# One core, a three-layer graph network: the engine and the place in the order at which edge attributes are split into bf16 parts

## The chip, the cores and the metric

The kernel runs on one core of a Trainium2 chip. The metric is the device time of one execution in microseconds. The kernel before takes 2959.71 us (median of three runs, 2949.01 to 2960.8).

## The reference

There are 12500 nodes with 64 features, and 212500 edges (200000 and one loop for each node), sorted by target `dst`, with 16 attributes each. Three layers of the same form are followed by a residual and a layer normalisation:

```python
def conv(h, W, b):
    m = jnp.concatenate([h[dst], h[src], edge_attr], axis=1) @ W + b
    return jax.ops.segment_sum(m, dst, num_segments=n_nodes)
h = relu(conv(x, W1, b1)); h = relu(conv(h, W2, b2)); h = conv(h, W3, b3)
out = layernorm(x + h)
```

Since `conv` is linear, a node needs three sums over its edges: of `h[src]`, of `edge_attr`, and the count. The sum of the attributes is the same in all three layers and is made once, in layer 0.

## The kernel before, in words

**Tiling.** The 12500 targets are 25 batches (`BATCHES`) of 500 nodes. Of a batch, 375 targets (`DENSE`) get their neighbours' sum as a product with a block of the adjacency matrix: for each of 100 tiles of 125 source nodes, `blocks[..., t, :]` holds the number of edges from those sources to the 375 targets in fp8. `apply_wide` (L1261) multiplies the high and middle bf16 parts of the features with it, `apply_narrow` (L1269) the low part; ten tiles are a unit. The remaining 125 targets ("far") are summed from gathered rows: 18 indirect DMAs of GpSimd (`gather_rows`, L712) fetch the source rows of 18 x 128 edges into `far_rows`, and `sum_far` (L1298, L1302) multiplies them with one-hot masks.

**Layer 0 builds the blocks.** While batch g is applied, batch g + 1 is built in 75 steps (`BUILDS`): VectorE makes a one-hot of 500 columns (`make_key`, L1018, a ring of 7 buffers), each fifth step also five small one-hots (`make_low`, L1008, two buffers), TensorE multiplies the two (`build_chunk`, L1241), and ScalarE copies the counts to fp8 (`keep_counts`, L796). Finished batches are stored to HBM (L804, 4.6 MB each) and read back in layers 1 and 2.

**Attributes.** In layer 0 each batch has six groups of edges, five near (75 targets, 128 x 11 edges) and one far (128 x 18 edges). SyncE loads a group's attributes and targets (`load_group`, four staging buffers), VectorE makes its mask (`make_mask`, L1026, `make_far_masks`, L1042), the fp32 attributes are split into three bf16 parts whose sum is the value, and TensorE sums them over the mask (`sum_attr`, L1288) after units 1, 3, 4, 6, 8 and 9. The split is `split_attr` on GpSimd, four instructions (L740 cast, L742 subtract, L744 cast, L746 subtract). It waits for the group's loads and for the sum two groups back, since `attr_parts` has two buffers. GpSimd's program alternates: a split, then three or four of the batch's 18 gathers (`GATHERS`).

**What orders VectorE.** Its program in layer 0 is one loop over the 75 steps n of the batch being built; small work for batches g and g - 1 is attached to fixed n: masks at 5, 25, 33, 48, 63, far masks at 18, 42, 57, `keep_acc` at 5 (it frees the PSUM bank that TensorE's next `apply_wide` waits for), `keep_attr` at 7, `keep_deg` at 12, `keep_h` at 32, and from 63 on the node steps: `take_nodes` (L1088) copies the convolution's result, four steps turn it into three parts.

**End of layer 0.** The gathers of layer 1 read rows of all nodes, so GpSimd waits for the stores of every batch's parts, the last of which follows batch 24's `sum_far`, its convolution and its node steps.

Of the kernel before, what the change touches and what calls it, by code (L numbers as in the profile page):

```python
# [5 lines left out]
def gnn_kernel(nc, x, src, dst, edge_attr, weights, out):  # L6
# [13 lines left out]
    ALU = mybir.AluOpType  # L20
# [4 lines left out]
    E, ED = edge_attr.shape  # L25
# [15 lines left out]
    NEAR = 5  # L41
    GW = DENSE // NEAR
    BUILDS = DENSE // W
# [12 lines left out]
    J = 11  # L56
    FJ = 18
    ROWS = [0, 112, L]
    PER_BATCH = NEAR + 1
# [24 lines left out]
    MASK_AT = [BUILDS * u // UNITS + 3 for u in SUM_AFTER[0:NEAR]]  # L84
    FAR_MASK_AT = [18, 42, 57]
    NODES_AT = [63, 66, 68, 70, 72]
    GATHERS = [FJ * k // NEAR for k in range(NEAR + 1)]
# [15 lines left out]
    with ctx:  # L103
# [432 lines left out]
        def landed_of(n):  # L536

            return sum(2 if m % PER_BATCH < NEAR else 1 for m in range(n % RING, n + 1, RING)) * DMA
# [133 lines left out]
        def _(pool):  # L672
# [58 lines left out]
            def split_attr(n):  # L731

                s, turn = n % RING, n % 2
                pool.wait_ge(attr_landed[s], landed_of(n))
                if n >= 2:
                    pool.wait_ge(attr_summed, n - 1)
                js = J if n % PER_BATCH < NEAR else FJ
                values = attr_stage[:, s, 0:js * ED].rearrange("p (j c) -> p j c", c=ED)
                into = [attr_parts[:, turn, 0:js, part * ED:(part + 1) * ED] for part in range(PARTS)]
                nc.gpsimd.tensor_copy(into[0], values).then_inc(attr_split, 1)  # L740
                pool.wait_ge(attr_split, n * PARTS + 1)
                nc.gpsimd.tensor_tensor(values, values, into[0], ALU.subtract).then_inc(attr_left, 1)  # L742
                pool.wait_ge(attr_left, n + 1)
                nc.gpsimd.tensor_copy(into[1], values).then_inc(attr_split, 1)  # L744
                pool.wait_ge(attr_split, n * PARTS + 2)
                nc.gpsimd.tensor_tensor(into[2], values, into[1], ALU.subtract).then_inc(attr_split, 1)  # L746

            for g in range(BATCHES):
                for k in range(PER_BATCH):
                    split_attr(g * PER_BATCH + k)  # L750
                    if k < NEAR:
                        for j in range(GATHERS[k], GATHERS[k + 1]):
                            gather_rows(g, j)
# [123 lines left out]
        def _(dve):  # L877
# [142 lines left out]

            def make_mask(b, k):
# [134 lines left out]
            for g in range(-1, BATCHES):  # L1156
                for n in range(BUILDS):
# [6 lines left out]
                    if g >= 0:  # L1164
                        if n == FIRST_MASK_AT:
# [280 lines left out]
```

## Time and profile before

| | |
|---|---|
| median of 3 runs | 2959.71 us |
| the profiled execution | 2963.69 us, its span 2961.8 us |
| mean granted TensorE clock | 0.981 |
| TensorE matmul busy | 2777.0 us, 94% of the span |
| VectorE busy | 1546.4 us, 52% |
| ScalarE busy | 1265.0 us, 43% |
| GpSimd busy | 2024.0 us, 68% |
| layer 0, steady batches | 200 to 1388 us of the span, 23 batches |

The busy shares are means over stages with different limits: VectorE is busy for nine tenths until about 1385 us and hardly at all later. Busy time of an instruction includes its end, which overlaps the next one's start, so start-to-start distances are shorter than durations. The stretch from 200 to 1388 us holds 23 of layer 0's 25 batches, from one `sum_far` to another.

### The profile page before, as it was taken

What the parts mean: (1) busy time and instruction counts of PE and PEld (TensorE: products, weight loads), DVE (VectorE), ACT (ScalarE), POOL (GpSimd) and SP (SyncE); (2) the same over time, 40 slices, a digit from 0 to 9 for tenths busy, and PEclk for the clock granted to TensorE, in tenths of its full rate; (3) what the DMA queues carried; (4) which work ended last, traced back from release to release, by engine and by line L of the source; (5) the groups of instructions that cost most, each with busy time, mean ns of one, the idle gap of its engine ahead of it and who ended that gap; (6) DMA issues with size and microseconds to landing.
All of it is one profiled execution on the core that took longest, in us unless ns stands there. A gap on an engine that the chain in (4) does not pass through costs nothing.

```text
span 2961.8 us, 60063 instructions
## 1 busy us (share of the span) xinstructions
PE 2777.0 (94%) x23143; PEld 1772.7 (60%) x23143; DVE 1546.4 (52%) x3237; ACT 1265.0 (43%) x2315; POOL 2024.0 (68%) x2141
## 2 busy tenths in 40 slices
PE   1499999999999999999859999999998999999998
PEld 0256666666666666666536666666665666666665
DVE  7999999999999999997201111111111212121211
ACT  2588898989889898986000000000000000000000
POOL 5277766676767767677277777777737777777773
PEclk9799999999999999999879999999999999999999
DMA  4353534445353444535958988888877899988882
GB/s 91 81 162 103 166 109 144 130 112 162 101 166 108 146 129 118 156 101 167 220 134 202 213 218 210 210 210 214 212 201 176 209 212 215 212 209 207 208 213 53
DMA packets 242618, 489.50 MB, mean 165 GB/s; under 512 B 156178, under 2 KB 191708, under 8 KB 214213
## 3 DMA queue, kind: packets, MB, share of 16 engines
q1 hardware_dynamic: 136846, 272.20, 34.8%
q10 hardware_dynamic: 58404, 143.10, 18.0%
q0 software_dynamic: 47088, 70.34, 12.2%
q8 instruction: 190, 3.11, 0.5%
q14 instruction: 90, 0.74, 0.1%
HBM read 341.80 MB, written 143.65 MB: 164 GB/s over the span
## 4 chain that ended last, share of the span: by engine, by line
PE 82%; DVE 5%; POOL 5%; issue 3%; DMA 2%; ACT 2%; SPq 1%; ACTq 0%; POOLq 0%; DVEq 0%
PE ps L1261 36%; PE ps L1269 20%; PE ps L1241 12%; POOL far_rows L712 4%; PE ps L1337 3%; PE ps L1298 3%; PE ps L1288 2%; PE ps L1338 2%; DVE is_key L1018 1%; PE ps L1302 1%; PE ps L1323 1%; ACT blocks L796 1%; DVE is_low L1008 1%; DMA parts<-in_x 1%; PE ps L1312 1%
## 5 line engine op out<-in xcount | busy, mean ns | idle before, releaser
L712 POOL DMA_INDIRECT far_rows<-parts,far_src x1350 | 1486.5, 1101 | 528.4 <-issue 382.1
L1261 PE MATMUL ps<-blocks,parts 125*128 125x375 fp8e4 x7500 | 1548.4, 324 | 4.0 <-ACT blocks L796 2.4
L796 ACT ACTIVATE blocks<-ps 125x505 fp8e4<-125x505 f32 x1875 | 1117.0, 756 | 149.0 <-PE ps L1241 146.2
L1261 PEld LDWEIGHTS ps<-blocks,parts 125*128 125x128 bf16 x7500 | 736.8, 100 | 421.3 <-issue 16.3
L1241 PE MATMUL ps<-is_key,is_low 128*125 128x505 bf16 x1875 | 707.9, 388 | 40.1 <-DVE is_key L1018 24.4
L1018 DVE TENSOR_SCALAR is_key<-from_one,parts 128x500 bf16<-128x500 f16 x1875 | 686.2, 413 | 3.0 <-PE ps L1241 1.2
L1269 PE MATMUL ps<-blocks,parts 125*64 125x375 fp8e4 x7500 | 686.6, 326 | 0.0
L1269 PEld LDWEIGHTS ps<-blocks,parts 125*64 125x64 bf16 x7500 | 399.0, 110 | 275.4 <-issue 154.4
L1115 DVE COPY z<-ps 125x256 f32<-125x256 f32 x51 | 21.6, 424 | 892.3 <-PE ps L1338 855.6
L1241 PEld LDWEIGHTS ps<-is_key,is_low 128*125 128x125 bf16 x1875 | 258.8, 139 | 226.8 <-DVE is_key L1018 51.5
L1042 DVE SCALAR_TENSOR_TENSOR far_masks<-far_dst,from_one 128x750 fp8e4<-128x750 int32 (+1 forms) x125 | 195.4, 1563 | 326.0 <-PE ps L1302 317.2
L1008 DVE TENSOR_TENSOR is_low<-from_one,parts 128x625 bf16<-128x625 f16 x375 | 307.1, 819 | 49.0 <-PE ps L1241 48.7
L740 POOL CAST attr_parts<-attr_stage 128x176 bf16<-128x176 f32 x150 | 72.1, 481 | 293.1 <-DMA dst_stage<-in_dst 150.2
L823 ACT ACTIVATE node_rows<-z,node_deg 125x64 f32<-125x64 f32 x200 | 54.0, 367 | 379.2 <-DVE z L1115 353.1
L855 ACT COPY acc_sb<-ps 128x500 f32<-128x500 f32 x50 | 28.8, 575 | 385.3 <-PE ps L1302 375.2
L863 ACT ACTIVATE std<-var,eps 125x4 f32<-125x4 f32 x25 | 7.4, 297 | 401.3 <-DVE var L1132 401.3
L857 ACT COPY own_sb<-ps 64x500 f32<-64x500 f32 x50 | 28.4, 568 | 279.9 <-PE ps L1323 279.9
L1298 PE MATMUL ps<-far_masks,far_rows 128*128 128x125 fp8e4 x1350 | 93.8, 224 | 51.2 <-DMA far_rows<-parts,far_src 51.2
L720 POOL TENSOR_SCALAR attr_stage<-attr_stage 128x256 f32<-128x256 f32 x150 | 136.9, 912 | 3.2
L1026 DVE SCALAR_TENSOR_TENSOR masks<-dst_stage,from_one 128x825 bf16<-128x825 int32 x125 | 128.9, 1032 | 8.4 <-DMA dst_stage<-in_dst 8.4
L1337 PE MATMUL ps<-w_src,acc_sb 128*125 128x64 f32 x600 | 124.0, 288 | 0.7 <-ACT own_sb L857 0.7
L1298 PEld LDWEIGHTS ps<-far_masks,far_rows 128*128 128x128 bf16 x1350 | 80.7, 100 | 68.4 <-issue 66.1
(120 smaller groups left out, 1423.2 us busy)
## 6 DMA issues: line engine op xcount, KB each, us to landing
blocks<-counts SPq DMA_DIRECT2D x100, 1066.4 KB
counts<-blocks ACTq DMA_DIRECT2D x25, 4101.6 KB
blocks<-counts SPq DMA_DIRECT2D x100, 984.4 KB
far_rows<-parts,far_src POOLq DMA_INDIRECT x1350
blocks<-counts SPq DMA_DIRECT2D x100, 123.8 KB
counts<-blocks ACTq DMA_DIRECT2D x25, 476.1 KB
blocks<-counts SPq DMA_DIRECT2D x100, 114.3 KB
attr_stage<-in_edge_attr SPq DMA_DIRECT2D x125, 88.0 KB, 1.9
```

The costliest lines, as they stand in the source:

```text
L712: nc.gpsimd.indirect_dma_start(far_rows[:, g % 2, j, :], None, parts_d[layer], bass.IndirectOffsetOnAxis(ap=far_src[:, g % BATCHES, j:j + ...
L720: nc.gpsimd.tensor_scalar(attr_stage[:, 3, 0:256], attr_stage[:, 1, 0:256], 1.0, None, ALU.mult).then_inc(rested, 1)
L796: nc.scalar.activation(blocks[0:L, b % 2, :, n * W:(n + 1) * W], build[0:L, c % BUILD, 0:COLS].rearrange("p (t w) -> p t w", w=W), ACT.Cop ...
L1008: nc.vector.tensor_tensor(is_low[:, m % 2, :, :], from_one[:, 0:L].rearrange("p (a l) -> p a l", a=1).to_broadcast([P, LOWS, L]), lows[:, ...
L1018: nc.vector.tensor_scalar(is_key[:, c % KEY_RING, 0:KEYS], from_one[:, :], keys[:, b, n:n + 1], None, ALU.is_equal).then_inc(keyed, 1)
L1026: nc.vector.scalar_tensor_tensor(out=masks[:, n % 2, :, :], in0=dst_stage[:, n % RING, :].rearrange("p (j a) -> p j a", a=1).to_broadcast( ...
L1042: nc.vector.scalar_tensor_tensor(out=far_masks[:, g % 2, js, :], in0=far_dst[:, b, js].rearrange("p (j a) -> p j a", a=1).to_broadcast(shape),
L1241: nc.tensor.matmul(build[0:L, c % BUILD, 0:COLS], is_low[:, c // LOWS % 2, c % LOWS, :], is_key[:, c % KEY_RING, 0:COLS], start=True, stop ...
L1261: nc.tensor.matmul(acc_ps(g), parts[0:L, layer % 2, t, 0:2, :].rearrange("p k d -> p (k d)"), blocks[0:L, g % 2, t, :], start=(t == 0), st ...
L1269: last = nc.tensor.matmul(acc_ps(g)[side:side + D, :], parts[0:L, layer % 2, t, 2, :], blocks[0:L, g % 2, t, :], start=False, stop=(t >= T ...
L1298: nc.tensor.matmul(acc_ps(g, at), far_rows[:, g % 2, j, 0:2 * D], far_masks[:, g % 2, j, :], start=(j == 0), stop=False)
L1337: nc.tensor.matmul(z_ps[:, t, :], acc_flat[:, at], w_src[layer][:, :], start=True, stop=False)
```

## The change

The four instructions of a split move from GpSimd to VectorE, one behind the one-hot of each of the steps n, n + 1, n + 2 and n + 3, where n is 1, 13, 22, 36, 45 or 58 (`SPLIT_AT`) for the six groups. The masks move to 5, 19, 28, 42, 54 and the far masks to 9, 30, 51. GpSimd's layer-0 program holds only the 25 x 18 gathers, which start as soon as their indices are loaded and the far rows two batches back are summed. The waits for loads and sums are kept, now on VectorE.

```diff
-    MASK_AT = [BUILDS * u // UNITS + 3 for u in SUM_AFTER[0:NEAR]]
-    FAR_MASK_AT = [18, 42, 57]
+    MASK_AT = [FIRST_MASK_AT, 19, 28, 42, 54]
+    FAR_MASK_AT = [9, 30, 51]
+    SPLIT_AT = [1, 13, 22, 36, 45, 58]
...
-            def split_attr(n):
-
-                s, turn = n % RING, n % 2
-                pool.wait_ge(attr_landed[s], landed_of(n))
-                if n >= 2:
-                    pool.wait_ge(attr_summed, n - 1)
...
             for g in range(BATCHES):
-                for k in range(PER_BATCH):
-                    split_attr(g * PER_BATCH + k)
-                    if k < NEAR:
-                        for j in range(GATHERS[k], GATHERS[k + 1]):
-                            gather_rows(g, j)
+                for j in range(FJ):
+                    gather_rows(g, j)
+            pool.wait_ge(attr_split, GROUPS * PARTS)
...
+            def split_high(n):
+                s = n % RING
+                dve.wait_ge(attr_landed[s], landed_of(n))
+                if n >= 2:
+                    dve.wait_ge(attr_summed, n - 1)
+                nc.vector.tensor_copy(attr_part(n, 0), attr_values(n)).then_inc(attr_split, 1)
+
+            def split_left(n):
+                dve.wait_ge(attr_split, n * PARTS + 1)
+                nc.vector.tensor_tensor(attr_values(n), attr_values(n), attr_part(n, 0), ALU.subtract).then_inc(attr_left, 1)
+
+            def split_mid(n):
+                dve.wait_ge(attr_left, n + 1)
+                nc.vector.tensor_copy(attr_part(n, 1), attr_values(n)).then_inc(attr_split, 1)
+
+            def split_low(n):
+                dve.wait_ge(attr_split, n * PARTS + 2)
+                nc.vector.tensor_tensor(attr_part(n, 2), attr_values(n), attr_part(n, 1), ALU.subtract).then_inc(attr_split, 1)
...
                     if g >= 0:
+                        if n in SPLIT_AT:
+                            split_high(g * PER_BATCH + SPLIT_AT.index(n))
+                        elif n - 1 in SPLIT_AT:
+                            split_left(g * PER_BATCH + SPLIT_AT.index(n - 1))
+                        elif n - 2 in SPLIT_AT:
+                            split_mid(g * PER_BATCH + SPLIT_AT.index(n - 2))
+                        elif n - 3 in SPLIT_AT:
+                            split_low(g * PER_BATCH + SPLIT_AT.index(n - 3))
```

On VectorE before, at the turn of a batch in layer 0, from the last node step (L1105) to `keep_acc` (L1053):

```order
L1105 TENSOR_TENSOR parts<-left,parts 125x4x64
L1018 TENSOR_SCALAR is_key<-from_one,parts 128x500 x2
L1008 TENSOR_TENSOR is_low<-from_one,parts 128x625
L1018 TENSOR_SCALAR is_key<-from_one,parts 128x500 x5
L1008 TENSOR_TENSOR is_low<-from_one,parts 128x625
L1018 TENSOR_SCALAR is_key<-from_one,parts 128x500
L1026 SCALAR_TENSOR_TENSOR masks<-dst_stage,from_one 128x825
L1072 TENSOR_REDUCE often<-blocks 125x1
L1053 COPY acc_sb<-ps 128x500
```

The same place on VectorE in the changed kernel, whose line numbers differ (L999 is `make_key`, L989 `make_low`, L1061 `keep_acc`, L1007 to L1019 the split):

```order
L989 TENSOR_TENSOR is_low<-from_one,parts 128x625
L999 TENSOR_SCALAR is_key<-from_one,parts 128x500 x2
L1007 CAST attr_parts<-attr_stage 128x11x16
L999 TENSOR_SCALAR is_key<-from_one,parts 128x500
L1011 TENSOR_TENSOR attr_stage<-attr_stage,attr_parts 128x176
L999 TENSOR_SCALAR is_key<-from_one,parts 128x500
L1015 CAST attr_parts<-attr_stage 128x11x16
L999 TENSOR_SCALAR is_key<-from_one,parts 128x500
L1019 TENSOR_TENSOR attr_parts<-attr_stage,attr_parts 128x11x16
L989 TENSOR_TENSOR is_low<-from_one,parts 128x625
L999 TENSOR_SCALAR is_key<-from_one,parts 128x500
L1034 SCALAR_TENSOR_TENSOR masks<-dst_stage,from_one 128x825
```

The four split instructions of the batch's first group stand between the one-hots ahead of the mask, the scan and `keep_acc`.

On GpSimd before, the start of layer 0's program (the far group's split and the gathers around it):

```order
L746 TENSOR_TENSOR attr_parts<-attr_stage,attr_parts 128x11x16
L712 DMA far_rows<-parts,far_src 128x192 x4
L740 CAST attr_parts<-attr_stage 128x18x16
L742 TENSOR_TENSOR attr_stage<-attr_stage,attr_parts 128x288
L744 CAST attr_parts<-attr_stage 128x18x16
L746 TENSOR_TENSOR attr_parts<-attr_stage,attr_parts 128x18x16
```

On GpSimd in the changed kernel, from the last index gather of the setup to the first pauses of layer 1:

```order
L690 DMA blocks<-in_src,blocks 125x256 x3
L690 DMA blocks<-in_dst,blocks 25x256
L712 DMA far_rows<-parts,far_src 128x192 x450
L720 TENSOR_SCALAR attr_stage<-attr_stage 128x256
L712 DMA far_rows<-parts,far_src 128x192 x6
```

All 450 gathers of layer 0 follow one another with nothing between them but their semaphores; no gather stands behind a split any more.

## Rows read from the trace of the kernel before

**Rows 1.** The page's first part: busy us, share of the span, instructions.

```profile
PE 2777.0 (94%) x23143; PEld 1772.7 (60%) x23143; DVE 1546.4 (52%) x3237; ACT 1265.0 (43%) x2315; POOL 2024.0 (68%) x2141
```

**Rows 2.** Windows: length, then busy us (count) of PE, PEld, DVE, ACT, POOL.

```profile
200.00:1388.00 1188.00, 1173.35 (x9438) 745.28 (x9439) 1103.38 (x2475) 1060.29 (x1908) 822.87 (x964) 1.00 0.46 132
1388.00:1480.00 92.00, 80.39 (x672) 50.69 (x671) 22.28 (x40) 5.14 (x19) 29.57 (x38) 0.89 0.97 232
1480.00:1567.00 87.00, 53.52 (x455) 35.33 (x454) 9.24 (x12) 4.31 (x12) 68.97 (x69) 0.82 0.62 147
```

**Rows 3.** Chain of waits, 652 to 658 us: start, length, what.

```profile
653.60 0.42 DVE z L1088
654.02 0.26 DVE is_key L1018
654.28 0.94 DVE is_low L1008
655.23 0.75 DVE is_key L1018
```

**Rows 4.** Timeline of TensorE at that place: start, length, what, idle before.

```profile
655.45 0.32 PE L1261 MATMUL ps<-blocks,parts 125*128 125x375 fp8e4 x1
656.02 0.43 PE L1241 MATMUL ps<-is_key,is_low 128*125 128x505 bf16 x1 [0.24 <-DVE is_key L1018]
```

**Rows 5.** Groups of instructions by form, 200 to 1388 us: count, busy us, mean ns, idle before.

```profile
L1018 DVE TENSOR_SCALAR is_key<-from_one,parts 128x500 bf16<-128x500 f16 x1719 | 634.2, 416 | 2.2 <-PE ps L1241 0.3
L1008 DVE TENSOR_TENSOR is_low<-from_one,parts 128x625 bf16<-128x625 f16 x343 | 281.3, 820 | 45.9 <-PE ps L1241 45.7
L1026 DVE SCALAR_TENSOR_TENSOR masks<-dst_stage,from_one 128x825 bf16<-128x825 int32 x115 | 118.6, 1031 | 0.0
L1101 DVE CAST parts<-left 125x256 bf16<-125x256 f32 x23 | 6.4, 280 | 0.0
L1105 DVE TENSOR_TENSOR parts<-left,parts 125x256 bf16<-125x256 f32 x23 | 9.4, 411 | 0.0
L712 POOL DMA_INDIRECT far_rows<-parts,far_src x413 | 506.0, 1225 | 108.8 <-issue 94.1 <-PE ps L1288 6.1
```

**Rows 6.** Timeline of VectorE in one steady batch.

```profile
661.58 1.55 DVE L1018 TENSOR_SCALAR is_key<-from_one,parts 128x500 bf16<-128x500 f16 x5
...
664.97 0.53 DVE L1072 TENSOR_REDUCE often<-blocks 125x1 f32<-125x375 uint8 x1
665.69 0.68 DVE L1053 COPY acc_sb<-ps 128x500 f32<-128x500 f32 x1 [0.20 <-PE ps L1302]
...
675.72 2.27 DVE L1018 TENSOR_SCALAR is_key<-from_one,parts 128x500 bf16<-128x500 f16 x5
...
685.43 0.80 DVE L1008 TENSOR_TENSOR is_low<-from_one,parts 128x625 bf16<-128x625 f16 x1
```

**Rows 7.** Timeline of GpSimd in the same batch.

```profile
675.76 0.49 POOL L740 CAST attr_parts<-attr_stage 128x176 bf16<-128x176 f32 x1 [3.00 <-PE ps L1288]
...
677.32 0.52 POOL L746 TENSOR_TENSOR attr_parts<-attr_stage,attr_parts 128x176 bf16<-128x176 f32 x1
...
686.15 0.79 POOL L740 CAST attr_parts<-attr_stage 128x176 bf16<-128x176 f32 x1 [4.00 <-DMA dst_stage<-in_dst]
```

**Rows 8.** Timeline of TensorE in batch 24, the last of layer 0.

```profile
1415.57 0.56 PE L1288 MATMUL ps<-masks,attr_parts 128*49 128x75 bf16 x11 [2.58 <-POOL attr_parts L746]
...
1429.83 1.20 PE L1288 MATMUL ps<-far_masks,attr_parts 128*49 128x125 fp8e4 x18 [2.81 <-POOL attr_parts L746]
1435.56 2.05 PE L1298 MATMUL ps<-far_masks,far_rows 128*128 128x125 fp8e4 x18 [4.53 <-DMA far_rows<-parts,far_src]
```

**Rows 9.** Timeline of GpSimd, batch 24 and the start of layer 1.

```profile
1411.62 0.33 POOL L740 CAST attr_parts<-attr_stage 128x176 bf16<-128x176 f32 x1 [6.27 <-DMA dst_stage<-in_dst]
...
1480.14 1.02 POOL L712 DMA_INDIRECT far_rows<-parts,far_src  x1 [49.63 <-issue]
```

**Rows 10.** Timeline of ScalarE's queue: the stores of batch 24's parts.

```profile
1455.01 0.98 ACTq L528 DMA_DIRECT2D parts<-parts  x2
```

More of the change, by code:

```diff
@@ L83, in gnn_kernel @@
     FIRST_MASK_AT = 5
-    MASK_AT = [BUILDS * u // UNITS + 3 for u in SUM_AFTER[0:NEAR]]
-    FAR_MASK_AT = [18, 42, 57]
+    MASK_AT = [FIRST_MASK_AT, 19, 28, 42, 54]
+    FAR_MASK_AT = [9, 30, 51]
+    SPLIT_AT = [1, 13, 22, 36, 45, 58]
     NODES_AT = [63, 66, 68, 70, 72]
-    GATHERS = [FJ * k // NEAR for k in range(NEAR + 1)]
     FAR_PIECE = FJ // len(FAR_MASK_AT)
@@ L729, in gather_batch @@
                     gather_rows(g, j)
-            def split_attr(n):
-                s, turn = n % RING, n % 2
-                pool.wait_ge(attr_landed[s], landed_of(n))
-                if n >= 2:
-                    pool.wait_ge(attr_summed, n - 1)
[L737 to L746, printed above, removed]
-            for g in range(BATCHES):
-                for k in range(PER_BATCH):
-                    split_attr(g * PER_BATCH + k)
-                    if k < NEAR:
-                        for j in range(GATHERS[k], GATHERS[k + 1]):
-                            gather_rows(g, j)
+            for g in range(BATCHES):
+                for j in range(FJ):
+                    gather_rows(g, j)
+            pool.wait_ge(attr_split, GROUPS * PARTS)
             for g in range(BATCHES, ALL):
@@ L1019, in make_key, with attr_values, attr_part @@
                                         None, ALU.is_equal).then_inc(keyed, 1)
+            def split_high(n):
[13 more added lines that the diff above has]
+                nc.vector.tensor_tensor(attr_part(n, 2), attr_values(n), attr_part(n, 1), ALU.subtract).then_inc(attr_split, 1)
+            def attr_values(n):
+                js = J if n % PER_BATCH < NEAR else FJ
+                return attr_stage[:, n % RING, 0:js * ED].rearrange("p (j c) -> p j c", c=ED)
+            def attr_part(n, part):
+                js = J if n % PER_BATCH < NEAR else FJ
+                return attr_parts[:, n % 2, 0:js, part * ED:(part + 1) * ED]
             def make_mask(b, k):
```

## The prediction, written before the changed kernel ran

> **What bounds the kernel now.** I read the page first: TensorE is busy for 94% of the span, VectorE for 52%, GpSimd for 68% [rows 1]. The means hide three stages, so I read the windows next. In layer 0's steady part (200 to 1388 us, 23 batches, so 51.7 us each) TensorE is busy for 1173 of 1188 us, VectorE for 1103, ScalarE for 1060, GpSimd for 823 [rows 2]. The reader is to see that TensorE bounds this stage and that VectorE has only 1188 - 1103 = 85 us of room, 3.7 us in a batch. From 1388 to 1567 us TensorE is busy for 134 of 179 us [rows 2]: there something else bounds, and this is where layer 0 hands over to layer 1. After that TensorE streams; nothing of the change is there.
>
> The chain of waits then says what still holds TensorE up in a steady batch. It runs along TensorE all the way but for one excursion [rows 3]: VectorE copies z, makes a one-hot, a set of small one-hots, and another one-hot, and TensorE takes that last one. The timeline of TensorE gives the price: an L1261 matmul starts at 655.45 and the next L1241 at 656.02, 0.57 us later [rows 4]. A matmul of 375 columns occupies TensorE for 375 / 2.4 GHz = 0.16 us at the full clock granted there [rows 2], so TensorE loses 0.41 us there. The profile marks only 0.24 us as idle because the matmul's modelled end covers the rest.
>
> Why is VectorE late at that place? Its last one-hot takes 0.75 us and the small ones 0.94 [rows 3], against means of 416 and 820 ns [rows 5]. Five one-hots on their own take 1.55 us, first start to last end, and 2.27 us where the GpSimd splits run (675.76 to 677.84) [rows 6, 7]. Start to start that is 1.47 and 2.19 us (the next row starts 0.08 us ahead of the end). So a split of GpSimd costs VectorE about 0.7 us, four instructions against five one-hots.
>
> **The change part by part.**
>
> *VectorE gains 24 instructions in a batch.* No row shows them at this size; the nearest are the node steps of 256 columns, a cast at 280 ns and a subtraction at 411 [rows 5]. Between 256 and 625 columns a two-input instruction grows by (820 - 411) / 369 = 1.1 ns a column [rows 5], so the subtraction of 176 columns is 411 - 80 x 1.1 = 0.32 us, and the far one of 288 is 0.45. The cast at 256 columns is cheaper than a subtraction, so I let it grow half as fast: 0.24 and 0.30 us; from above it can cost what the subtraction does. Five near groups at 2 x (0.24 + 0.32) and one far at 2 x (0.30 + 0.45) are 7.1 us of duration; each overlaps its neighbour by 0.08 us, so VectorE's time grows by 7.1 - 24 x 0.08 = 5.2 us, at most 6.2. I take 5.2, the value nearest to the cast's own row.
>
> The Trainium skill (Advanced Engine Details and Errata, § VectorE Performance Modes) lets a cast use both read ports only where the outer dimensions of source and target are both even, or odd and equal. By that rule a near cast, 176 columns into 11 x 16, could run at one element a cycle; the sum would be the upper end. No row of before shows such a shape: the node cast's outer dimension is even.
>
> *VectorE loses the delays that the splits cause.* Six splits a batch at 0.7 us are 4.2 us. The other bound is all that one-hots lose today: a mean of 416 ns [rows 5] against 0.34 undisturbed (0.26 us start to start [rows 3], and 0.08 of overlap), 76 ns x 75 = 5.7 us. A part of that is from the gathers, which stay. I take 4.5 us.
>
> The Trainium skill (SBUF — State Buffer, § Who interferes with whom) says why: VectorE and GpSimd share a port pair, and whichever starts first keeps it for its whole instruction. The trace agrees, a one-hot waits 0.4 us for a GpSimd subtraction of 0.52 us. The same section has GpSimd's descriptor writing use that pair too, which speaks against the change: the gathers keep some delays alive and now come in one run.
>
> *Balance on VectorE:* 48.0 us busy in a batch today (1103 / 23), 48.0 + 5.2 - 4.5 = 48.7 after, under 51.7. TensorE stays the bound, and the new instructions cost nothing by themselves. Between the ends it is 47.5 to 50.0. If the relief did not come at all, it would be 53.2 to 54.2 (below, rival C).
>
> *The stall behind z.* Undisturbed, z, one-hot, small one-hots, one-hot take 0.34 + 0.26 + 0.72 + 0.34 = 1.66 us, so the one-hot is ready at 655.26 and TensorE wants it at 655.61. The stall goes: 23 x 0.41 = 9.4 us off. What is late next is `keep_acc`, for which TensorE's next wide matmul waits. Today VectorE reaches it 0.20 us before `sum_far` is done [rows 6]. From z (653.60) to that arrival (665.49) are 11.9 us. The work in them, start to start: z 0.34, 17 one-hots at 0.26, four small sets at 0.74, four node steps 1.06, the mask 0.95, the scan 0.45, in all 10.2, so 1.7 us are delays. The change puts one split in (0.8 us, at most 1.0) and takes the GpSimd splits' delays out: 11.0 plus what the gathers cost. Available, once the stall is gone, are 12.09 - 0.41 = 11.7 us. Margin 0.7 us; a gather's delays must stay under that. Bounds of this term: 9.4 off, and 0 (all of it comes back at `keep_acc`).
>
> *New waits on VectorE.* The split at step 36 waits for the fourth group's load, which lands at 686.1 behind the store of the counts; GpSimd waits 4.0 us for it today [rows 7]. VectorE begins step 35 at 685.43 [rows 6], so it gets there at about the landing. Queued behind the split are the next one-hots, for which TensorE waits; but the ring holds seven, 7 / 75 of a batch or 4.8 us of TensorE's work, against a wait of at most 2 us. Nothing. The waits for `attr_summed` at 36 and 58 fall where the ring is full anyway. SyncE's loads wait for splits and masks, both of which now come earlier than the masks do today.
>
> *Gathers.* 18 at 1.225 + 0.3 us are 27 us of a 51.7 us batch [rows 5], issued one batch ahead: hidden. In the last batch this pays. Layer 0's batch 24 has no building beside it, and TensorE waits three times [rows 8]: 2.58 us for the split of the group that lands at 1411.6, 2.81 us for the far group's split, 4.53 us for the gathers, which GpSimd could issue only behind the splits. Afterwards the gathers are long in. After the landing VectorE makes the split, now alone (four dependent steps, 1.3 us), and the mask (1.0): ready at 1413.9, where today it is 1415.4, so 1.5 us off. The far split is ready by 1419, before it is needed: 2.8 off. The gathers: 4.5 off. Together 8.8 us.
>
> Does the rest follow? `sum_far`, convolution, node steps, the store of the parts at 1455.0 [rows 10], and GpSimd's first gather of layer 1 at 1480.1 after 49.6 us of waiting [rows 9] are one serial chain. Only the store's 25 us lie in a crowded stretch (DMA share 0.97 [rows 2]); its landing could gain less, or more. I take 8.8, between 0 and 14.
>
> *Start.* In batch 0 the first loads land before VectorE needs them. Nothing, give or take 1 us.
>
> **Sum.** 9.4 + 8.8 = 18.2 us off the profiled 2963.69: 2945.5. That execution lies 4 us above the median shown; from the median it is 2959.71 - 18.2 = 2941.5 us. I give that.
>
> **Rivals.** (A) Both terms, 2941.5, between 2929 and 2948.
> (B) Only one term comes. Either `keep_acc` takes the stall's place, since the gathers now run through the window from z to it, or the store of the last parts lands when the queues let it. For it: a margin of 0.7 us, a DMA share of 0.97. Against it: away from the splits five one-hots took 1.47 us [rows 6]. Saved 9 us or less: about 2951 to 2960.
> (C) Slower: VectorE becomes layer 0's bound. It decides from 3.7 us of added time a batch. If the one-hots' delays came from the gathers and stay, VectorE needs 48.0 + 5.2 = 53.2 us a batch, 1.5 more than TensorE: 23 x 1.5 = 34 us, less 8.8 at the end: about +25, 2985 us. At the upper end of the split's cost it is 23 x 2.5 - 8.8 = +49, 3008. Against it: rows 6 and 7 put the delays beside the splits.
> (D) More: at the handover TensorE's clock, 0.89 and 0.82 of full [rows 2], stays up and the store lands sooner; another 6 us or more, under 2929.
>
> **Chances.** A 0.54, B 0.27, C 0.14, D 0.05. This kernel's measurement tells a change from none at about 0.5%, 15 us. A above its upper part and D are faster by over 0.5%: 0.57. Its upper edge and B are within: 0.29. C is slower: 0.14. The range that leaves out C and most of D is 2925 to 2966 us.
>
> **What would show it.** Right: VectorE's one-hots at a mean near 350 to 360 ns, its busy time near 48.7 us a batch, the batch at 51.3 us, no TensorE wait for a one-hot behind z, in batch 24 no waits for the far split and the gathers, layer 1's first gather near 1462. Wrong: a batch longer than 51.7 us with TensorE waiting for one-hots (C); `keep_acc` starting later than `sum_far`'s end (B); one-hots still above 400 ns; split casts above 0.32 us; the first gather of layer 1 less than 9 us earlier than the steady part's gain explains.

## The result, and the profile after

The changed kernel took 2939.83 us (median of 5 runs, 2936.8 to 2942.02) and the kernel before 2959.71 us beside it (2949.01 to 2965.32): ratio 0.9943, 95% interval 0.9923 to 0.9963. The forecast was 2941.5 us. The profiled execution took 2942.02 us against 2963.69, so 21.7 us are to be found between two traces; the forecast's sum was 18.2.

The page's first part and the windows of the changed kernel (length, busy us of PE, PEld, DVE, ACT, POOL, granted clock, DMA share, GB/s), which answer to [rows 1, 2]:

```profile
PE 2766.1 (94%) x23143; PEld 1771.1 (60%) x23143; DVE 1579.2 (54%) x3837; ACT 1265.4 (43%) x2315; POOL 1690.0 (57%) x1541
```

```profile
200.00:1384.00 1184.00, 1171.40 (x9472) 748.93 (x9470) 1127.99 (x3029) 1060.61 (x1909) 520.54 (x414) 1.00 0.47 133
1388.00:1480.00 92.00, 74.78 (x666) 47.83 (x664) 25.51 (x57) 4.26 (x16) 16.02 (x17) 0.92 0.98 233
1480.00:1567.00 87.00, 68.37 (x580) 44.96 (x580) 11.37 (x13) 5.46 (x14) 69.45 (x68) 0.86 0.67 163
```

VectorE has 600 instructions more and is busy for 1128 / 23 = 49.0 us of a steady batch (before 48.0), GpSimd for 22.6 instead of 35.8. TensorE still bounds the steady part.

To place the 21.7 us I take the first `sum_far` matmul of each batch as its mark, counting from the first one, batch 0. All times in us:

| stretch | before | after | gained |
|---|---|---|---|
| start to mark 0 | 198.2 | 199.4 | -1.2 |
| mark 0 to mark 23 (23 steady batches) | 1190.0 | 1184.4 | 5.6 |
| mark 23 to mark 24 | 47.3 | 35.4 | 11.9 |
| mark 24 to the store of the last parts | 19.5 | 14.2 | 5.3 |
| that store to layer 1's first gather | 25.1 | 27.4 | -2.2 |
| the rest | | | 2.3 |

Each number is rounded by itself. The rest lies in layers 1 and 2, and what made it was not traced.

Groups of VectorE and GpSimd in the steady part (by form: count, busy us, mean ns, idle before), answering to [rows 5]:

```profile
L999 DVE TENSOR_SCALAR is_key<-from_one,parts 128x500 bf16<-128x500 f16 x1719 | 556.9, 355 | 0.8
L989 DVE TENSOR_TENSOR is_low<-from_one,parts 128x625 bf16<-128x625 f16 x343 | 276.5, 806 | 16.7 <-PE ps L1257 13.6
L1011 DVE TENSOR_TENSOR attr_stage<-attr_stage,attr_parts 128x176 f32<-128x176 f32 x115 | 38.1, 332 | 0.0
L1007 DVE CAST attr_parts<-attr_stage 128x176 bf16<-128x176 f32 x115 | 37.6, 327 | 0.0
L1007 DVE CAST attr_parts<-attr_stage 128x288 bf16<-128x288 f32 x23 | 7.3, 317 | 0.0
L712 POOL DMA_INDIRECT far_rows<-parts,far_src x414 | 521.1, 1259 | 668.9 <-DMA far_src<-in_src 549.7 <-issue 119.2
```

One-hots fell from 416 to 355 ns. The near cast of 176 columns is no shorter than its subtraction, and the far cast of 288 columns is shorter than the near one. GpSimd's gathers no longer wait their turn behind splits but for their indices, 24 us in each batch.

Now the steady batches. 8 of the 23 take 51.20 to 51.26 us, 15 take 51.56 to 51.77. The last of the 23 is one of those; it is longer in most kernels here, whether or not `keep_acc` is late. In the other 14, called late batches from here on, `keep_acc` starts 0.36 to 0.51 us later behind `sum_far` than in the rest. A late batch, VectorE's and then GpSimd's and TensorE's timelines (start, length, what, idle before), answering to [rows 3, 6]:

```profile
292.08 0.42 DVE L1096 COPY z<-ps 125x256 f32<-125x256 f32 x1 [0.81 <-PE ps L1354]
292.43 0.51 DVE L999 TENSOR_SCALAR is_key<-from_one,parts 128x500 bf16<-128x500 f16 x1
...
294.09 0.49 DVE L1100 TENSOR_SCALAR parts<-z 125x256 bf16<-125x256 f32 x1
...
303.77 0.53 DVE L1080 TENSOR_REDUCE often<-blocks 125x1 f32<-125x375 uint8 x1
304.23 0.66 DVE L1061 COPY acc_sb<-ps 128x500 f32<-128x500 f32 x1
```

```profile
291.88 0.95 POOL L712 DMA_INDIRECT far_rows<-parts,far_src  x1 [0.30 <-issue]
293.13 1.33 POOL L712 DMA_INDIRECT far_rows<-parts,far_src  x1 [0.30 <-issue]
```

```profile
301.86 1.20 PE L1314 MATMUL ps<-far_masks,far_rows 128*128 128x125 fp8e4 x18
...
305.03 1.13 PE L1277 MATMUL ps<-blocks,parts 125*128 125x375 fp8e4 x6 [0.35 <-DVE acc_sb L1061]
```

From z to `keep_acc` VectorE needs 304.23 - 292.08 = 12.15 us; in a batch in time `keep_acc` can start 11.64 us behind z, when TensorE has the sum ready. The one-hot of 0.51 us, beside a gather that runs on, is one of several instructions that are longer than on their own in this window. A batch in time looks so, VectorE and then GpSimd:

```profile
653.39 0.42 DVE L1096 COPY z<-ps 125x256 f32<-125x256 f32 x1 [1.24 <-PE ps L1354]
653.73 0.34 DVE L999 TENSOR_SCALAR is_key<-from_one,parts 128x500 bf16<-128x500 f16 x1
...
665.02 0.68 DVE L1061 COPY acc_sb<-ps 128x500 f32<-128x500 f32 x1 [0.45 <-PE ps L1318]
```

```profile
653.33 0.94 POOL L712 DMA_INDIRECT far_rows<-parts,far_src  x1 [0.30 <-issue]
...
655.94 1.24 POOL L712 DMA_INDIRECT far_rows<-parts,far_src  x1 [0.30 <-issue]
```

Eight gathers run in either window. Here the row ahead of `keep_acc` ends 665.02 - 0.45 - 653.39 = 11.18 us behind z, and since rows overlap by 0.08 us, `keep_acc` could start at 11.1 us; arrivals below are given so. The reader is to see that the two batches run the same instructions and differ in how gathers and one-hots fall on each other.

Batch 24 on TensorE, answering to [rows 8]:

```profile
1408.44 0.57 PE L1304 MATMUL ps<-masks,attr_parts 128*49 128x75 bf16 x11
...
1418.11 1.19 PE L1304 MATMUL ps<-far_masks,attr_parts 128*49 128x125 fp8e4 x18
1419.24 1.20 PE L1314 MATMUL ps<-far_masks,far_rows 128*128 128x125 fp8e4 x18
1420.37 0.69 PE L1318 MATMUL ps<-far_masks,far_rows 128*64 128x125 fp8e4 x18
1421.88 1.61 PE L1277 MATMUL ps<-blocks,parts 125*128 125x375 fp8e4 x9 [0.82 <-issue]
...
1424.38 2.60 PE L1277 MATMUL ps<-blocks,parts 125*128 125x375 fp8e4 x15
```

All three waits are gone. VectorE's split there and layer 1's first gather, answering to [rows 9]:

```profile
1405.49 0.34 DVE L1007 CAST attr_parts<-attr_stage 128x176 bf16<-128x176 f32 x1 [8.37 <-DMA dst_stage<-in_dst]
```

```profile
1460.77 1.00 POOL L712 DMA_INDIRECT far_rows<-parts,far_src  x1 [47.24 <-issue]
```

The same matmuls behind `sum_far` in the kernel before, and the windows around them:

```profile
1439.51 2.98 PE L1261 MATMUL ps<-blocks,parts 125*128 125x375 fp8e4 x9 [0.82 <-issue]
...
1444.19 4.39 PE L1261 MATMUL ps<-blocks,parts 125*128 125x375 fp8e4 x15
```

```profile
1418.00:1419.00 1.00, 1.00 (x4) 0.30 (x2) 0.00 (x0) 0.00 (x0) 0.88 (x1) 0.50 0.84 158
1430.00:1431.00 1.00, 1.00 (x18) 0.84 (x15) 0.00 (x0) 0.00 (x0) 0.51 (x1) 0.93 0.76 149
1432.00:1436.00 4.00, 0.45 (x5) 0.48 (x6) 0.00 (x0) 0.00 (x0) 0.00 (x0) 0.50 1.11 264
1444.00:1448.00 4.00, 4.00 (x15) 2.04 (x15) 0.16 (x1) 1.06 (x4) 0.00 (x0) 0.51 1.03 193
1448.00:1452.00 4.00, 4.00 (x41) 2.91 (x40) 2.95 (x2) 0.00 (x0) 0.00 (x0) 1.00 0.96 189
```

Before, TensorE ran at the lower of its two levels (0.50, 1.2 GHz) through the 4.53 us wait, which began at 1431.0, and until 1448. The row of 1430 to 1431 has a mean of 0.93 with TensorE busy throughout: the clock fell just ahead of that wait, 1.0 us after work had resumed behind the wait of 2.81 us [rows 8]. So the last wait by itself need not be what lowered it. Nine wide matmuls took 2.98 us instead of 1.61, fifteen 4.39 instead of 2.60. With `sum_far` itself (3.1 us from first start to last end, after 1.8) and the degrees' matmuls (1.84 and 1.03 us) that is 1.4 + 1.8 + 1.3 + 0.8 = 5.3 us, the whole gain of that line of the table.

### The profile page after: what moved, and what is told of

Read it like the earlier page. It is cut to its first block, busy times and chain, and to the rows that moved or that the text cites. A ratio compares the mean times of both kernels' runs of the same rounds, so it can differ in the third digit from the quotient of the medians.

```text
span 2940.2 us, 60063 instructions
## 1 busy us (share of the span) xinstructions
PE 2766.1 (94%) x23143; PEld 1771.1 (60%) x23143; DVE 1579.2 (54%) x3837; ACT 1265.4 (43%) x2315; POOL 1690.0 (57%) x1541
## 4 chain that ended last, share of the span: by engine, by line
PE 82%; DVE 9%; issue 3%; POOL 3%; DMA 1%; ACT 1%; SPq 1%; ACTq 0%; POOLq 0%; DVEq 0%
PE ps L1277 38%; PE ps L1285 20%; PE ps L1257 11%; PE ps L1353 3%; DVE is_key L999 3%; PE ps L1314 2%; POOL far_rows L712 2%; PE ps L1354 2%; PE ps L1304 2%; DVE is_low L989 2%; PE ps L1339 1%; PE ps L1318 1%; ACT blocks L777 1%; DMA parts<-in_x 1%; PE ps L1328 1%
## 5 line engine op out<-in xcount | busy, mean ns | idle before, releaser
L1277 PEld LDWEIGHTS ps<-blocks,parts 125*128 125x128 bf16 x7500 | 734.3, 99 | 425.9 <-issue 10.9
L999 DVE TENSOR_SCALAR is_key<-from_one,parts 128x500 bf16<-128x500 f16 x1875 | 606.4, 355 | 2.4 <-PE ps L1257 1.6
L1123 DVE COPY z<-ps 125x256 f32<-125x256 f32 x51 | 21.7, 425 | 892.9 <-PE ps L1354 892.9
L989 DVE TENSOR_TENSOR is_low<-from_one,parts 128x625 bf16<-128x625 f16 x375 | 302.2, 806 | 18.0 <-PE ps L1257 14.9
L1353 PEld LDWEIGHTS ps<-w_src,acc_sb 128*125 128x125 f32 x600 | 88.5, 187 | 47.4 <-issue 43.7
```

Of the source, the lines that this page charges most:

```text
L989: nc.vector.tensor_tensor(is_low[:, m % 2, :, :], from_one[:, 0:L].rearrange("p (a l) -> p a l", a=1).to_broadcast([P, LOWS, L]), lows[:, ...
L999: nc.vector.tensor_scalar(is_key[:, c % KEY_RING, 0:KEYS], from_one[:, :], keys[:, b, n:n + 1], None, ALU.is_equal).then_inc(keyed, 1)
L1277: nc.tensor.matmul(acc_ps(g), parts[0:L, layer % 2, t, 0:2, :].rearrange("p k d -> p (k d)"), blocks[0:L, g % 2, t, :], start=(t == 0), st ...
L1353: nc.tensor.matmul(z_ps[:, t, :], acc_flat[:, at], w_src[layer][:, :], start=True, stop=False)
```

## The experiments

All were measured beside the kernel before on the same chip (its median was 2957.5 to 2960.1); 1 to 4, 5 to 8 and 9 to 11 each shared its runs. Ratios are to that kernel.

**1. The first split later.** Of the changed kernel:

```
-    SPLIT_AT = [1, 13, 22, 36, 45, 58]
+    SPLIT_AT = [6, 13, 22, 36, 45, 58]
```

> The changed kernel with the first group's split at steps 6 to 9 instead of 1 to 4, so that it stands behind keep_acc. Theory (in 12 of 23 steady batches the stall that left the place behind z came back at keep_acc, because VectorE has one more split and the gathers' collisions between z and keep_acc): all steady batches take 51.2 us instead of 51.2 to 51.7, the first layer is 12 x 0.45 = 5 us shorter than in the changed kernel, some 2935 us against 2940; no TensorE wait for acc_sb. Rival (the 51.7 us batches come from ScalarE or from the stores): the same mix of 51.2 and 51.7, 2940 us.

Measured: 2934.81 us, ratio 0.9928 (0.9912 to 0.9943). 22 of 23 steady batches take 51.20 to 51.26 us, 1178.6 us in all (after: 1184.4). The meetings with gathers remain: a one-hot of 0.49 to 0.50 us lies ahead of `keep_acc` in each of the first 22 batches, but with a split's work less VectorE arrives 10.9 us behind z.

**2. Gathers in their own batch.** Of the changed kernel; a batch's gathers wait until the batch before is summed:

```
-                    if g >= 2:
+                    if 1 <= g < BATCHES:
+                        pool.wait_ge(far_summed, g)
+                    elif g >= 2:
```

> The changed kernel with the 18 gathers of a batch issued at the start of that batch (they wait for the far sum one batch back, not two), so that none runs between z and keep_acc. Theory (it is the gathers' collisions with VectorE's instructions that make keep_acc late): steady batches 51.2 us, one-hots beside z at 0.34 us; about 5 us less in the steady part. At the end of layer 0 the gathers of batch 24 share the queues with the store of the counts and the loads; they still land before 1419, so the end stays within 2 us of the changed kernel's: 2935 us. Rival (the split alone, 1 us, fills the margin): the batches stay mixed, 2940. Second rival: the gathers delay the fourth group's load, VectorE waits at step 36, and the end of layer 0 gives 2 to 5 us back.

Measured: 2940.27 us, ratio 0.9946 (0.9931 to 0.996). All batches take 51.2 us, with no gather between z and `keep_acc`, and VectorE arrives at 11.1 to 11.2 us with the split in place: the lateness is the gathers'. But mark 23 to 24 takes 41.6 us instead of 35.4; TensorE waits 1.9 us for gathered rows and 2.5 for a mask in batch 24. What the steady part won, the end gave back, as the second rival had it: the group's load lands 24.8 us behind mark 23 instead of 21.7, and the mask waits for it.

**3. Gathers ahead, splits left on GpSimd.** Of the kernel before:

```
+            for j in range(FJ):
+                gather_rows(0, j)
             for g in range(BATCHES):
                 for k in range(PER_BATCH):
                     split_attr(g * PER_BATCH + k)
-                    if k < NEAR:
-                        for j in range(GATHERS[k], GATHERS[k + 1]):
-                            gather_rows(g, j)
+                    if k >= 3 and g + 1 < BATCHES:
+                        for j in range((0, 5, 10)[k - 3], (5, 10, FJ)[k - 3]):
+                            gather_rows(g + 1, j)
```

> The kernel before with the gathers alone moved one batch ahead; the splits stay on GpSimd. Theory (the end of layer 0 was held up by gathers that stood behind the splits, the steady batch by the splits' collisions): steady batches stay at 51.67 us with the 0.41 us stall behind z; in batch 24 the wait for the gathers (4.5 us) goes, those for the splits (2.6 and 2.8 us) stay, the store of the last parts is issued 5 to 9 us sooner after the batch's start, and the kernel is 5 to 9 us faster than before, about 2952. Rival (the end's gain came from TensorE having no waits at all in batch 24 and so keeping its clock): only the 4.5 us or less, 2955 or more, with the granted clock still down between 1404 and 1444 us.

Measured: 2956.82 us, ratio 1.0004 (0.9994 to 1.0014). No gain, but two things cancel in the trace: mark 0 is 14.9 us later, since batch 0's 18 gathers stand ahead of its first split, and mark 23 to layer 1's first gather is 77.5 us instead of 91.9. The theory had the waits for the two splits stay in batch 24; they are gone too, but for 0.9 us at the first, although the splits are still GpSimd's, and mark 23 to 24 takes 36.5 us. So those waits hung on the gathers between the splits, not on the engine that splits. One-hots stay at 423 ns: their relief in the changed kernel is from the splits, not from the gathers' place.

**4. The casts walked the other way.** Of the changed kernel, 16 x 11 in place of 11 x 16, through `rearrange("p j c -> p c j")` on both operands:

> The changed kernel with the two casts of a split walked column by column (16 x 11 instead of 11 x 16 elements), the same data. The Trainium skill (Advanced Engine Details and Errata, VectorE Performance Modes) lets a cast use both read ports where the outer dimensions are both even, or odd and equal; the near cast took 327 ns at 176 columns, no less than the subtraction at 332. By that rule the near cast drops to about 240 ns, VectorE has 0.9 us more room in a batch and keep_acc is late in fewer batches: 2936 us. Rival (the short rows or the two types cost the second element, not the outer dimension): the cast stays at 327 ns or gets longer, 2940 us or more. Second rival: it gets shorter, but as a two-port instruction now waits for the gathers, and nothing is gained.

Measured: 2935.95 us, ratio 0.9935 (0.992 to 0.995). The casts became longer, not shorter, by form:

```profile
L1010 DVE CAST attr_parts<-attr_stage 128x176 bf16<-128x176 f32 x115 | 65.6, 570 | 0.0
L1010 DVE CAST attr_parts<-attr_stage 128x288 bf16<-128x288 f32 x23 | 19.4, 843 | 0.0
```

and still 22 of the 23 batches take 51.2 to 51.3 us: VectorE arrives 11.3 to 11.6 us behind z in them. The two longer casts are 0.5 us of duration there, but the one-hot behind such a cast starts 0.23 us after it, so the pair adds only 0.2 us to VectorE's time in the window. Meetings of the late batches are few: one one-hot of 0.55 us in five batches, where the late ones above have several such delays. So it isn't VectorE's sum of work that makes a batch late, but the phase in which gathers meet its instructions. Why this walk keeps them apart I did not find out. The expectation's 240 ns, which it took from the rule, is refuted: walked so, both outer dimensions are 16 here, and the cast takes 1.7 times as long.

**5. The changed kernel again,** unedited.

> The changed kernel itself, unedited, beside the other three on the same chip. Theory: 2940 us again, with more than half of the 23 steady batches at 51.6 to 51.7 us and keep_acc 0.36 to 0.52 us late in them; which batches are late may differ from the first profile, because it hangs on where the gathers fall. Rival: the late batches were one execution's accident, and a second profile has all of them at 51.2.

Measured: 2939.14 us, ratio 0.9931 (0.9917 to 0.9946). 9 of the first 22 batches are late by 0.35 to 0.52 us, in another pattern (the first profile: 14). Lateness is a habit of the kernel, its count one of the execution. "More than half" was too many.

**6. The look behind `keep_acc`.** `look` is the reduction of 0.53 us ahead of `keep_acc` (L1080). Of the changed kernel (batch 0 keeps its look where it was):

```
                         if n == FIRST_MASK_AT:
                             make_mask(g, 0)
-                            look(g)
 ...
                             keep_acc(g - 1)
+                            look(g)
```

> The changed kernel, with the reduction look(g), 0.45 us start to start, moved from ahead of keep_acc to behind it. Theory: what was lost in a late batch is the arrival at keep_acc, 12.0 to 12.14 us behind z where 11.64 are to be had. With 0.45 us of work less ahead of it, VectorE arrives after 11.55 to 11.7: the late batches go from 51.6 to 51.7 down to 51.2 to 51.3, and the time to 2935 us, 5 below the changed kernel, though the gathers stand where they stood and one-hots in that window still take up to 0.55 us. Rival: TensorE waits there for the gathered rows or for the far mask, not for keep_acc; then the late batches stay and the time is 2940.

Measured: 2936.25 us, ratio 0.9919 (0.9905 to 0.9934), 2.9 below the run before beside it. The meetings remain, in fewer batches (five of the first 22); VectorE arrives 11.54 to 11.56 us behind z in four of them, which fits into 11.64, and at 11.68 in the fifth. VectorE in one of them:

```profile
394.63 0.42 DVE L1096 COPY z<-ps 125x256 f32<-125x256 f32 x1 [1.20 <-PE ps L1356]
...
396.50 0.49 DVE L1100 TENSOR_SCALAR parts<-z 125x256 bf16<-125x256 f32 x1
...
406.27 0.68 DVE L1061 COPY acc_sb<-ps 128x500 f32<-128x500 f32 x1
```

The same 0.49 us step as in the late batch above, yet `keep_acc` starts 1.86 us behind the start of `sum_far`, as in every batch that is in time. The rival, that TensorE waited there for gathered rows or the far mask, is refuted.

**7. One gather more in each batch.** The kernel before; from batch 18 on the gathers run a batch ahead:

```
+                        until = FJ * g + GATHERS[k + 1] + min(g, FJ)
+                        while issued < min(until, FJ * (g + 1) if k < 3 else FJ * BATCHES):
+                            gather_rows(*divmod(issued, FJ))
+                            issued += 1
```

> The kernel before, splits on GpSimd as they were, but GpSimd issues one gather more in each batch than it uses, so that from batch 18 on the gathers run a whole batch ahead; the start is as before. Theory: the end of layer 0 gains by the gathers alone. Batch 24 no longer waits for them, the clock of TensorE stays up there, and the tail from batch 23 to layer 1's first gather is 77 us in place of 92: 2943 us, 14 to 15 below before, with the steady batches still 51.7 us and one-hots at a mean of 415 to 425 ns. Rival: the tail's gain needs the splits on VectorE, since batch 24's waits of 2.6 and 2.8 us for GpSimd splits remain and the clock falls as before: 2953 us, 4.5 below.

Measured: 3011.48 us, ratio 1.0193 (1.0165 to 1.022). A miss by my schedule: it puts 14 gathers between splits 3 and 4. GpSimd in one batch:

```profile
1360.71 1.41 POOL L740 CAST attr_parts<-attr_stage 128x176 bf16<-128x176 f32 x1 [7.68 <-PE ps L1291]
...
1384.57 0.95 POOL L712 DMA_INDIRECT far_rows<-parts,far_src  x1 [0.30 <-issue]
1385.51 0.35 POOL L740 CAST attr_parts<-attr_stage 128x176 bf16<-128x176 f32 x1
```

The next split starts some 20 us later than it would behind no gathers, and batches go to 58 us. The end gains as expected even so (mark 23 to layer 1's first gather 75.3 us).

**8. VectorE busier.** Experiment 1's kernel with

```
+            def spare_work():
+                dve.wait_ge(spared, spares[0])
+                nc.vector.tensor_reduce(spare[:, :], ident[:, :], axis=X, op=ALU.add).then_inc(spared, 1)
+                spares[0] += 1
 ...
+                        if any(0 <= n - at <= 4 for at in SPLIT_AT):
+                            spare_work()
```

> The changed kernel with the first split at step 6 (as in the first experiment), and at each split five reductions of 128 fp32 columns more on VectorE, into a number nobody reads: 30 in a batch. At 0.15 to 0.25 us each, start to start, they are 4.5 to 7.5 us a batch. VectorE has 2.7 us of idle time in a batch there. Theory: the first 2.7 us cost nothing, and what is above lengthens the batch: 1.8 to 4.8 us in each of 24, 2976 to 3045 us, with TensorE waiting for one-hots. Rival: VectorE's order is so tight beside TensorE's that each addition costs from the start, 4.5 to 7.5 us a batch and 3040 to 3110 us. Other rival: the ring of one-hots and the waits behind it leave more room than the idle time says, and the time stays under 2960.

Measured: 3021.38 us, ratio 1.0212 (1.0197 to 1.0227). By form, and what TensorE's weight loads wait for now:

```profile
L1015 DVE TENSOR_REDUCE spare<-ident 128x1 f32<-128x128 f32 x491 | 135.5, 276 | 0.0
```

```profile
PEld ps L1268 <- DVE is_key L1001: 101.0, 164, 1.6
```

30 x (0.276 - 0.08) = 5.9 us a batch, less 2.7 of idle time, is 3.2; batches are 54.79 us, 3.6 more. This is what the forecast's rival C describes, made on purpose: above its room VectorE bounds, about one for one.

**9. The same as 7, spread.** At most 3 gathers behind each of splits 0 to 2, the others behind splits 3, 4 and 5 at 5 : 5 : 8 (until batch 9 that is 3, 3, 3, 3, 3, 4).

> The kernel before with its splits on GpSimd and one gather more issued in each batch than it uses, as in the run by steps, but the gathers spread: from batch 18 on 5, 5 and 8 of the next batch behind splits 3, 4 and 5, where that run had 14 in one row between splits 3 and 4 and its batches went to 58 us. Theory: that row held the splits up; spread, the steady batches stay at 51.7 us and the end of layer 0 gains as it did there and in the run with gathers ahead (batch 23 to the first gather of layer 1 in 75 to 78 us, before: 92). So the gathers' place alone, without a split moved, brings 14 to 16 us: ratio 0.995, some 2945 us beside 2959.7. Rival: the splits on GpSimd suffer from any gather ahead, and the batches come out at 52 us or more from batch 10 on, which eats the 14 us: ratio 0.998 or above.

Measured: 2941.86 us, ratio 0.9951 (0.9937 to 0.9964). The gathers' place in GpSimd's order, no split moved, is worth about as much as the whole change; the two intervals overlap. Mark 23 to 24 takes 36.5 us, then 14.2 to the store. But the steady part gained too, 1184.8 us, which neither theory had: eight of the first nine batches take 51.2 to 51.3 us (one 51.8, with no wait behind z). GpSimd in the kernel before, and in this one, around z:

```profile
652.78 0.43 POOL L740 CAST attr_parts<-attr_stage 128x288 bf16<-128x288 f32 x1
...
654.64 1.17 POOL L746 TENSOR_TENSOR attr_parts<-attr_stage,attr_parts 128x288 bf16<-128x288 f32 x1
```

```profile
338.01 0.44 POOL L740 CAST attr_parts<-attr_stage 128x288 bf16<-128x288 f32 x1
...
340.48 0.73 POOL L746 TENSOR_TENSOR attr_parts<-attr_stage,attr_parts 128x288 bf16<-128x288 f32 x1
```

Before, the far split covers 652.8 to 655.8, right on z and its one-hots (z at 653.60 [rows 3]). Here it is over at 341.2 and z comes at 342.46: the one-hot behind z takes 0.34 us and the small set 0.80, and the stall is gone with the splits still on GpSimd and one-hots at a mean of 420 ns. This holds for the first nine of the 23 only. As more gathers are issued ahead, the far split moves later against z. In the tenth it reaches z, in the next three it lies on z as before, and the stall is back; TensorE in the eleventh, with z at 753.15:

```profile
755.57 0.43 PE L1247 MATMUL ps<-is_key,is_low 128*125 128x505 bf16 x1 [0.25 <-DVE is_key L1024]
```

In the last ten it starts 1.3 to 3.0 us behind z, and they take 51.4 to 51.9 us, with a wait of up to 0.36 us for a one-hot 6.2 us behind z in some. So within one kernel the stall goes and comes with the far split's place.

**10. Experiments 1 and 6 together.**

> The changed kernel with both cures at once: first split at step 6 and the look behind keep_acc. Theory: each of them alone already brings all batches to 51.2 us, which is TensorE's own work; so the second brings nothing: 2934 to 2936 us, ratio 0.992. Rival: VectorE's time ahead of keep_acc still costs TensorE something that the late arrivals don't show; then it is 2931 or less.

Measured: 2934.56 us, ratio 0.9925 (0.9911 to 0.9939). No further gain, though VectorE now arrives 1.1 us or more ahead of the 11.64: VectorE's work ahead of `keep_acc` doesn't hold the batch at 51.2 us. Experiments 1, 4, 6 and 10 are the best versions and not told apart.

**11. A wait made in batch 24.** Experiment 1's kernel, 64 reductions ahead of the far split there:

```
+                        if g == BATCHES - 1 and n == SPLIT_AT[5]:
+                            for m in range(64):
+                                spare_work(m)
```

> The changed kernel with its first split at step 6, and in batch 24 alone 64 reductions of 128 columns on VectorE ahead of the far group's split, into a number nobody reads, at about 0.28 us each: the far split is late by 18 us, of which some 6 us are hidden, so TensorE waits 11 to 12 us for it. Theory: what gave the end of layer 0 its further 5 us is the clock. A wait of this length lowers TensorE's granted clock behind it, as the kernel before shows after its 2.8 and 4.5 us waits (0.67 in 1424 to 1444 us), and the stretch from sum_far to the store of the parts takes 17 to 20 us in place of 14.2; the time is that of the first experiment, 2934.8, plus 11.5 plus 3 to 5 us: 2949 to 2952. Rival: the stretch was longer before for another reason (the DMAs beside it, the splits on GpSimd); then it stays at 14.2 us and the time is 2946.

Measured: 2949.98 us, ratio 0.9977 (0.9969 to 0.9986). The total is the theory's, but not its parts: TensorE waited 15.0 us and mark 24 came 16.0 later, while the stretch to the store took 15.1 us, 0.9 more and not 3 to 5. Windows:

```profile
1411.00:1413.00 2.00, 0.00 (x0) 0.00 (x0) 1.79 (x7) 0.00 (x0) 0.00 (x0) 1.00 1.07 236
1414.00:1426.00 12.00, 0.03 (x1) 0.06 (x2) 10.78 (x38) 0.00 (x0) 0.09 (x1) 0.50 0.27 67
1426.00:1430.00 4.00, 4.00 (x38) 3.63 (x40) 2.27 (x6) 1.06 (x4) 0.77 (x1) 0.50 0.31 77
1431.00:1435.00 4.00, 3.48 (x23) 2.36 (x24) 0.58 (x2) 0.61 (x3) 0.00 (x0) 1.00 0.95 274
```

The clock does fall in a wait and outlasts it, but here it rose about 4 us after work resumed at 1425.97; before, it stayed low for 12 us after 1435.56, behind a wait a third as long. In whole, the clock was low for 17.1 us in both kernels, from 1413.0 to 1430.1 here and from 1430.9 to 1447.9 before. What differs is how much of it fell on work: here it began 2 us into a wait of 15.0, before just ahead of one of 4.53. So the long wait took most of the low stretch into itself. The low stretch behind the wait of 2.58 us at 1415.57 was 3.4 us, and no run shows what sets the length.

## Why the prediction was right

The time was right within 2 us, and the sum within 3.5. That is in part luck. The batches gave 5.6 us for 9.4 forecast, the end of layer 0 (mark 23 to layer 1's first gather) 15.0 for 8.8, the start -1.2 for nothing, and another 2.3 lie where nothing was forecast. The mechanisms named were there: the stall behind z went, and so did the three waits of batch 24. The sizes were off in opposite directions.

*VectorE's splits.* Near cast 0.327 us for 0.24, near subtraction 0.332 for 0.32, far ones 0.31 and 0.45 for 0.30 and 0.45. In all 10 x 0.66 + 2 x 0.76 - 1.9 = 6.2 us a batch: the upper end, not the 5.2 that I took. The forecast had beside it the Trainium skill's rule on outer dimensions (Advanced Engine Details and Errata, § VectorE Performance Modes), and these rows agree with it: 11 x 16 runs like a subtraction, 18 x 16 is shorter although it has more columns. I held to the node cast, whose shape differs. The rule doesn't give the price of every walk: in experiment 4 both outer dimensions are even, and the cast took 570 ns.

*Relief.* 61 ns x 75 = 4.6 us on one-hots for 4.5. Experiment 3 confirms its source. (The one-hot beside the subtraction of 0.52 us was 0.68 us long, 0.34 more than on its own, where the forecast says that it waits 0.4.) With masks and small sets shorter too, VectorE is at 49.0 us a batch; 48.7 was forecast, and the mean batch is 51.5 us for 51.3.

*The stall behind z.* Gone in every batch. It was worth more than 9.4: where nothing replaces it (experiment 1) the 23 batches fall from 1190.0 to 1178.6, 11.4 us. A usual batch falls by 0.46 us, 0.41 was forecast; the rest is from three longer batches of before. What was mis-sized is the step behind it, "Margin 0.7 us; a gather's delays must stay under that". Without delays VectorE now arrives at 11.1 us of 11.64, so 0.54 us was the margin, and gathers in a bad phase add 0.9 to 1.0. The forecast has no size for these delays in the changed order. Rival B's first half is thus true in some 9 to 14 batches, and 5.8 of the 11.4 us came back. Experiments 1, 2 and 6 take away the split, the gathers or the look from that window, and each of them ends it.

*The end of layer 0.* 11.9 us to mark 24 instead of 8.8. The waits were worth 9.9, not 8.8: of the first, 2.58 us, the forecast let 1.1 stand, but the group's load landed 21.7 us behind mark 23 and not 23.4, and the wait went whole. The low clock behind it (0.50 at 1418) had cost the work up to the far split's wait another 1.8 us, which I had not counted: 11.45 us of it before, 9.67 after. The remaining 0.2 are spread. Another 5.3 us are the low clock behind `sum_far`'s start: the first half of rival D, which I gave 0.05. Experiments 3, 7 and 9 show the short stretch with splits on GpSimd, and experiment 11 a lengthened one after a wait. The store's landing gave 2.2 us back, rival B's second half; it takes 25.1 us before and 25.8 to 28.9 in the other twelve traces, and two executions of the changed kernel differ by 1.6, so how much of this is the change's is not shown.

*Layer 1's first gather* at 1460.8 for "near 1462" is right because 3.8 us less than forecast in the batches and 1.2 less at the start are made up by 6.2 more at the end.

*What the reasons missed.* The forecast took both terms for consequences of moving the splits. Experiment 9 leaves them where they were and reaches 0.9951, an interval that overlaps the change's. What the stall needed was that the far split not lie on z, by a shift (it ended 2.2 us behind z's start, and 1.3 us ahead of it in experiment 9's early batches) or by taking it off GpSimd; what the end needed was gathers a batch ahead. The forecast has two of batch 24's waits end because VectorE splits; experiment 3 ends them with GpSimd splitting. The move has its own use when it is placed well: 2934.8 us, below the 2941.9 of experiment 9. But 14 of experiment 9's batches are not at their best, and a kernel with splits on GpSimd, gathers ahead and the far split clear of z in every batch was not run.

Open: why the gathers fall in or out of phase, why the turned casts keep them in, what sets the length of a low clock, whether the store's landing depends on the change, and what the 2.3 us in layers 1 and 2 are.

## What to carry to other kernels

A delay that one engine's work adds to another's costs only where it lands on the one short chain that the bound engine waits for; look for what runs beside that chain before moving work off an engine, since a shift in order can do as much. When a wait goes, work out the margin at the next one, take from it every instruction that may meet a neighbour there in its worst phase, and move what isn't urgent (a split, a reduction) behind it. In a drained last stage, price a wait with the clock behind it, and keep such a price wide.

## What the runs showed of the hardware

- A VectorE cast from fp32 to bf16 took 327 ns for 11 x 16 and 301 to 317 for 18 x 16. Walked across the rows (16 x 11 and 18 columns deep), 570 to 578 and 833 to 843 ns: 3.2 to 3.3 and 2.9 ns a column. The one-hot behind such a near cast started 0.23 us after it and took 0.46 us; the two together were 0.11 us longer than with the straight walk.
- In a late batch one-hots took up to 0.55 us and gathers 0.94 or 1.33; in a batch in time one-hots took 0.34 to 0.35 and gathers 0.94 to 1.24. Both patterns were stable over several batches. The Trainium skill says that whoever starts first keeps the shared port for its whole instruction (SBUF — State Buffer, § Who interferes with whom). The rows agree with it only in part: the one-hot at 292.43 started within a gather's issue of 0.95 us and took 0.51 us, but the one at 653.73 started within one of 0.94 us and took 0.34, and neither of these two was longer than on its own. What part of a gather's issue holds the port no run shows.
- The granted clock fell to 0.50 2 us into a wait of 15.0 us and rose 4 us after it; in the kernel before it fell just ahead of a wait of 4.53 us and was still low 12 us after it. The low stretch was 17.1 us long in both.
